# Storing the attention's numerators and sums undivided, features on partitions, and dividing in the output stage

## The chip, the cores and the metric

One core of one Trainium2 chip. The metric is the device time of one execution in microseconds: the median of three runs, and beside it one profiled execution from which all rows below come. Five engines matter: TensorE (matmuls and transposes, PE in the profile, PEld its weight loads), VectorE (DVE), ScalarE (ACT), GpSimd (POOL), and SyncE (SP), which issues all DMAs of this kernel.

## The reference

A transformer block on x of 16 batches, 512 rows, 128 features: 16 heads of 8 features, relative positions clipped at 20, then a gated feed-forward part.

```python
# q, k, v: layernorm(x) @ W.T + b, per head; rk2, rv2: rel_k, rel_v by clipped distance
attn1 = jnp.einsum('bhqd,bhkd->bhqk', q, k)
attn2 = jnp.einsum('bhqd,qkd->bhqk', q, rk2)
attn = jax.nn.softmax((attn1 + attn2) / scale, axis=-1)
w1 = jnp.einsum('bhqk,bhkd->bhqd', attn, v)
w2 = jnp.einsum('bhqk,qkd->bhqd', attn, rv2)
out = (w1 + w2).transpose(0, 2, 1, 3).reshape(B, S, E) @ Wo.T + bo
x = x + out
h = jax.nn.silu(gate) * up          # of layernorm(x)
x = x + h @ wd.T
```

## The kernel before

Three stages run one after the other, each a block that all engines leave together: projections (to about 200 us), attention (to about 1216 us) and output (to the end). Between them, queries, keys, values and the attention's result go through memory.

The attention stage (`stage_attend`) works in 64 units: 16 batches of 4 blocks of 128 query rows; i = 0 to 3 is the block within the batch. A unit has 8 score chunks c, two for each of the 4 key blocks t = c // 2, each chunk of two banks of 512 columns. TensorE writes scores to three banks `b_s` in turn, ScalarE takes the exponential of each bank (L1004, `b_p<-b_s`). Before each bank TensorE waits for `p_ready` of the exponential that frees it, three banks back; in `scores`, where t == i (the diagonal block), it waits for each of the two banks by itself and issues the first bank's work and the row-maximum scores before the second wait, otherwise it waits once for both. Beside each chunk stand the row-maximum scores of two heads of the unit after next (L810, `b_a<-k,q`), whose maxima VectorE takes (L1043).

The unit before is finished during the chunks of the present one. c = 0: the last value products (L901, `b_pv`). c = 1: relative values into the bank `b_mi` (L916), masked by VectorE (L1050, `b_wm`). c = 2: their sums into `b_pv` (L927); ScalarE copies `b_pv` to `b_xt` (L1016), and behind it the transposed guard rows to `b_mt` (L1010). After chunk 3: `output_transposes`, four transposes of `b_xt` back into `b_mi` (L937); VectorE divides: reciprocal of the 16 sums (L1057) and a product (L1062) into `b_xn`; SyncE stores `b_xn` (L721) at the end of its unit, two units behind. In SyncE's queue, per unit: with i = 0 and 1 operand loads of the next batch (L231), each held until a chunk of scores is done; the guard rows of the next unit (L683, two DMAs); more operand loads; with i = 2 the values; then the store.

The output stage (`stage_output`) takes one batch per step, with projection of the batch after. TensorE per step: output projection of the next batch (L1164, `c_py`), three pairs of gate and up products (L1181, L1182), the attention's transposes of the batch after next (L1156, `c_pa`), 12 down products (L1189), transposes of the next batch's normalised rows (L1172). ScalarE copies the transposed attention to `c_aT` (L1220), which the projection reads, and takes the Silu (L1235). VectorE: residual sum (L1251), statistics, hidden products 0 and 1 (L1271), normalisation (L217), hidden product 2, final sum (L1288). GpSimd: the deviation's inverse and the bias addition of the batch after next (L1132). Loads for the batch after next are issued by SyncE once the residual sum has been made.

Of the kernel before, what the change touches and what calls it, by code (L numbers as in the profile page):

```python
# [16 lines left out]
P = 128  # L17
# [38 lines left out]
NQ4 = 4  # L56
# [539 lines left out]
def stage_attend(nc, m, k, d):  # L596
# [18 lines left out]
    names = ("init", "a_ready", "a_used", "half", "s_ready", "p_ready", "w_ready", "w_masked", "pv_ready", "xt_ready", "rd",  # L615
             "mp_ready", "mt_ready", "mt_copied", "xtt_ready", "norm", "m_in",
# [6 lines left out]
    NSR = 2 * SUB  # L623
    NQD = HP * QB
# [50 lines left out]
    with nc.Block() as block:  # L675
        @block.sync
        def _(sp):
# [18 lines left out]

            def unit(at):
# [10 lines left out]
                if at.plus(1).exists():  # L708
                    guard_rows(at.plus(1))
                if ahead:  # L710
                    for c in range(3, (SUB, NLOAD - SUB)[i]):
                        chunk(c)
                        operands(first, range(c + SUB * i, c + SUB * i + 1))
                if i == 2 and at.since(T) and at.plus(T).exists():
                    load_values(sp, k, d, at.it * 2 + at.c // T + 1, (at.c // T + 1) % 2)
                if at.count() == 4 * T:
                    for p in range(2):
                        sp.wait_ge(xo_out[p], 16 * T)
# [8 lines left out]
            for u in (U - 2, U - 1):  # L727
                sp.wait_ge(s["norm"], u + 1)
                sp.dma_start(d["xo"][u], XN[u % 2][:, :]).then_inc(xo_out[u % 2], 16)
# [70 lines left out]
        def _(pe):  # L800
# [133 lines left out]
            def output_transposes(at):  # L934
                pe.wait_ge(s["xt_ready"], at.count(1, 1))
                for g in range(NQ4):
                    ins = nc.tensor.transpose(MI[:, g * P:(g + 1) * P], XT[:, g * P:(g + 1) * P], k["ident"][:, :])  # L937
                ins.then_inc(s["xtt_ready"], 1)

# [40 lines left out]
            pe.wait_ge(s["norm"], U - 1)  # L980
            relative_values(end)
            relative_value_sums(end)
            output_transposes(end)

        @block.scalar
        def _(act):
# [45 lines left out]
        def _(dve):  # L1032
# [21 lines left out]
            def normalise(at):  # L1054
                dve.wait_ge(s["xtt_ready"], at.count(1, 1))
                v = MI[:, :].rearrange("p (n c) -> p n c", c=32)
                nc.vector.reciprocal(RD[:, :], v[:, :, HD]).then_inc(s["rd"], 1)  # L1057
                dve.wait_ge(s["rd"], at.count(1, 1))
                if at.since(2):
                    dve.wait_ge(xo_out[at.c % 2], at.even(1) * 16)  # L1060
                xn = XN[at.c % 2][:, :].rearrange("p (a g d) -> p g a d", a=NQ4, d=HD)
                nc.vector.tensor_tensor(xn, MI[:, :].rearrange("p (g a c) -> p g a c", g=NQ4, a=NQ4)[:, :, :, 0:HD],  # L1062
                                        bc(RD[:, :].rearrange("p (g a) -> p g a", g=NQ4), 3, HD), ALU.mult).then_inc(s["norm"], 1)

# [17 lines left out]
            normalise(end)  # L1082
# [8 lines left out]
def stage_output(nc, m, k, d):  # L1091
# [3 lines left out]
    XA, X, x_in = k["xa"], k["x"], k["rows_in"]  # L1095
    X1 = [m.sb(f"c_x1{p}", [P, T, E]) for p in range(2)]
    XNT = [m.sb(f"c_xnT{p}", [P, S]) for p in range(2)]
    xn, fin, aT = m.sb("c_xn", [P, T, E]), m.sb("c_fin", [P, T, E]), m.sb("c_aT", [P, S])
# [3 lines left out]
    pA, pT, py, po = (m.ps(f"c_p{n}", [P, S]) for n in ("a", "t", "y", "o"))  # L1102
    PG, PU = ([m.ps(f"c_p{n}{p}", [P, S]) for p in range(2)] for n in "gu")
    names = ("xb", "aT", "aTs", "y", "x1", "var", "eps", "rstd", "xn", "xT", "xTs", "gate", "up", "silu", "hid",
# [6 lines left out]
    with nc.Block() as block:  # L1111
        @block.sync
        def _(sp):
            def step(at):
                if at.plus(2).exists():
                    sp.wait_ge(s["x1"], at.count(1, 1))
                    if at.count() == 0:
                        for p in range(2):
                            sp.wait_ge(k["xo_out"][p], 16 * U // 2)
# [8 lines left out]
        def _(pool):  # L1128
            def biased(at):
                x = X[at.c % 2]  # L1130
                pool.wait_ge(x_in[at.c % 2], at.even(1) * 32 + 32)
# [4 lines left out]

            biased(at0(0))
# [12 lines left out]
        def _(pe):  # L1150
            def attention_transposes(at):
                pe.wait_ge(x_in[at.c % 2], at.even(1) * 32 + 32)
                if at.since(1):
                    pe.wait_ge(s["aTs"], at.count())
                for t in range(T):
                    ins = nc.tensor.transpose(pA[:, t * P:(t + 1) * P], XA[at.c % 2][:, t, :], k["ident"][:, :])  # L1156
                ins.then_inc(s["aT"], 1)

            def output_projection(at):
                pe.wait_ge(s["aTs"], at.count(1, 1))  # L1160
                if at.since(1):
                    pe.wait_ge(s["x1"], at.count())
                for t in range(T):
                    ins = nc.tensor.matmul(py[:, t * P:(t + 1) * P], aT[:, t * P:(t + 1) * P], k["wo"][:, :], start=True, stop=True)  # L1164
# [29 lines left out]
            attention_transposes(at0(0))  # L1194
            output_projection(at0(0))
            attention_transposes(at0(1))
            row_transposes(at0(0))

            def step(at):
# [5 lines left out]
                if at.plus(2).exists():  # L1205
                    attention_transposes(at.plus(2))
# [8 lines left out]
        def _(act):  # L1215
            def transposed_attention(at):
                act.wait_ge(s["aT"], at.count(1, 1))
                if at.since(1):
                    act.wait_ge(s["y"], at.count())
                nc.scalar.copy(aT[:, :], pA[:, :]).then_inc(s["aTs"], 1)  # L1220

# [4 lines left out]
            transposed_attention(at0(0))  # L1226
            transposed_attention(at0(1))
            transposed_rows(at0(0))

            def step(at):  # L1230
# [5 lines left out]
                if at.plus(2).exists():  # L1236
                    transposed_attention(at.plus(2))
# [6 lines left out]
        def _(dve):  # L1244
# [27 lines left out]

            residual(at0(0))
            normalise(at0(0))

            def step(at):
# [7 lines left out]
                hidden(at, 2)  # L1284
                dve.wait_ge(s["down"], at.count(1, 1))
# [8 lines left out]
def program(nc, d):  # L1294
    for name, shape, dt in (("qop", (B, PARTS, P, S), BF16), ("kop", (B, PARTS, P, S), BF16),
                            ("v", (B, P, S), F32), ("guard", (B, P, VGW - VW), F32), ("xo", (U, P, E), F32)):
# [57 lines left out]
```

## Time and profile before

| | |
|---|---|
| median of 3 runs | 1385.82 us (1384.87 to 1387.82) |
| the profiled execution | 1384.85 us, span 1383.1 us |
| TensorE busy | 1264.9 us, 91% |
| VectorE busy | 955.0 us, 69% |
| ScalarE busy | 757.8 us, 55% |
| GpSimd busy | 551.3 us, 40% |
| DMA | 79.08 MB, mean 57 GB/s |

A busy share is a mean over three stages of different kind. The page cuts the span in 40 slices of 34.6 us and gives the busy tenths of each; slices 1 to 5 are the projections, 7 to 35 attention, the last five the output stage. A row of the timeline is an instruction or a run of equal ones, with its start and length and, in brackets, how long its engine had been idle and what it waited for. A row of the groups has count, busy time, and the mean length in nanoseconds.

### The profile page before, as it was taken

Reading aid. Unit: us, or ns where it says so; the run is one execution under the profiler, and the core shown is the slowest. Engines: PE = TensorE matmul, PEld = TensorE weight load, DVE = VectorE, ACT = ScalarE, POOL = GpSimd, SP = SyncE. Lnnn points to the kernel's source line nnn. Section 1 sums busy time; section 2 is a strip of 40 time slices with the busy share of each in tenths; the row PEclk is TensorE's granted clock in tenths of the full one; section 3 lists DMA queues with packets and bytes.
Section 4 is the critical chain, followed back from the end, with each engine's and each line's share of the span. In section 5 each row is a group of like instructions: output and inputs, shape, how many; then the busy total and the mean of one; then the engine's idle time right before and its main releaser. Section 6 shows DMA issues by size and latency. Waiting matters only on the chain. (4 is left out here: it accounts for less than half of the span.)

```text
span 1383.1 us, 67607 instructions
## 1 busy us (share of the span) xinstructions
PE 1264.9 (91%) x30680; PEld 937.8 (68%) x30688; DVE 955.0 (69%) x1844; ACT 757.8 (55%) x1413; POOL 551.3 (40%) x983
## 2 busy tenths in 40 slices
PE   4387669999999999999999999999999999979998
PEld 3254437777777777777777777777777777756766
DVE  6499876776766767677767676676777776146664
ACT  4367525565655656555656566565666565623332
POOL 4376623443435343434344343534344443122221
PEclk9789959999999999999999999999999999989999
DMA  4544520111020112011111101111211110113231
GB/s 126 141 168 167 179 60 7 42 33 55 23 55 23 52 32 57 21 54 42 33 49 29 55 20 54 30 47 32 56 35 41 45 32 9 41 41 92 69 92 46
DMA packets 101541, 79.08 MB, mean 57 GB/s; under 512 B 13256, under 2 KB 97032, under 8 KB 101256
## 3 DMA queue, kind: packets, MB, share of 16 engines
q1 hardware_dynamic: 101256, 74.77, 18.3%
q8 instruction: 242, 3.96, 1.3%
q14 instruction: 43, 0.35, 0.1%
HBM read 45.90 MB, written 27.26 MB: 53 GB/s over the span
## 5 line engine op out<-in xcount | busy, mean ns | idle before, releaser
L1043 DVE TENSOR_REDUCE b_mx<-b_a 128x1 f32<-128x512 f32 x1024 | 658.7, 685 | 234.0 <-PE b_a L810 228.7
L1004 ACT ACTIVATE b_p<-b_s 128x512 f32<-128x512 f32 x1024 | 569.8, 595 | 399.3 <-PE b_s L851 313.6
L901 PE MATMUL b_pv<-b_p,vg 128*16 128x128 f32 x8192 | 286.7, 275 | 0.1
L774 POOL TENSOR_TENSOR qd<-q,one 48x512 bf16<-48x512 bf16 x256 | 266.2, 1040 | 28.7 <-POOLq L286 3.8
L751 POOL TENSOR_TENSOR b_np<-vg,one 128x16 bf16<-128x16 f32 x192 | 39.1, 264 | 560.7 <-DVE b_mx L1043 550.4
L851 PE MATMUL b_s<-qd,z 112*128 112x32 bf16 (+1 forms) x6016 | 248.8, 189 | 0.7 <-issue 0.6
L810 PE MATMUL b_a<-k,q 48*128 48x512 bf16 x1024 | 202.8, 393 | 26.8 <-DVE b_mx L1043 11.3
L851 PEld LDWEIGHTS b_s<-qd,z 112*128 112x128 bf16 x6016 | 205.8, 99 | 11.0 <-issue 1.0
L901 PEld LDWEIGHTS b_pv<-b_p,vg 128*16 128x16 f32 x8192 | 196.2, 96 | 21.4 <-issue 0.6
L836 PE MATMUL b_s<-q,k 54*128 54x64 bf16 (+3 forms) x4608 | 188.2, 201 | 6.4 <-issue 2.5
L836 PEld LDWEIGHTS b_s<-q,k 54*128 54x128 bf16 (+1 forms) x4608 | 126.4, 95 | 92.4 <-PE b_s L836 29.2
L810 PEld LDWEIGHTS b_a<-k,q 48*128 48x128 bf16 x1024 | 49.7, 94 | 95.9 <-ACT b_p L1004 39.8
L861 PE MATMUL b_s<-q,k 118*128 118x64 bf16 x2048 | 104.4, 194 | 0.7 <-issue 0.7
L861 PEld LDWEIGHTS b_s<-q,k 118*128 118x128 bf16 x2048 | 76.8, 98 | 30.0 <-issue 30.0
L1050 DVE TENSOR_TENSOR b_wm<-b_mi,wmask 128x512 f32<-128x512 f32 x64 | 44.3, 692 | 65.8 <-PE b_mi L916 65.8
L927 PE MATMUL b_pv<-b_wm,red 128*16 128x128 f32 x2048 | 70.3, 274 | 5.4 <-DVE b_wm L1050 4.9
L916 PE MATMUL b_mi<-b_p,tvd 128*32 128x64 f32 x4096 | 70.6, 221 | 0.0
L362 PE MATMUL a_pr<-relbd,a_parts 128*128 128x320 bf16 x128 | 29.7, 316 | 37.2 <-DVE a_gr L572 37.2
L916 PEld LDWEIGHTS b_mi<-b_p,tvd 128*32 128x32 f32 x4096 | 60.3, 110 | 4.6
L1235 ACT ACTIVATE c_sg<-c_pg 128x512 f32<-128x512 f32 x48 | 28.7, 597 | 54.8 <-PE c_pg L1181 54.8
L927 PEld LDWEIGHTS b_pv<-b_wm,red 128*16 128x16 f32 x2048 | 50.7, 96 | 11.6 <-DVE b_wm L1050 7.7
L362 PEld LDWEIGHTS a_pr<-relbd,a_parts 128*128 128x128 bf16 x128 | 11.8, 111 | 62.7 <-DVE a_gr L572 53.1
(125 smaller groups left out, 1321.8 us busy)
## 6 DMA issues: line engine op xcount, KB each, us to landing
x<-in_x SPq DMA_DIRECT2D x32, 256.0 KB, 3.2
scratch_qop<-a_parts SPq DMA_DIRECT2D x16, 384.0 KB, 2.5
scratch_kop<-a_parts SPq DMA_DIRECT2D x16, 384.0 KB, 3.2
k<-scratch_kop SPq DMA_DIRECT2D x32, 192.0 KB
q<-scratch_qop SPq DMA_DIRECT2D x32, 192.0 KB
scratch_v<-a_vr SPq DMA_DIRECT2D x16, 256.0 KB, 3.2
k<-scratch_kop SPq DMA_DIRECT2D x32, 128.0 KB
q<-scratch_qop SPq DMA_DIRECT2D x32, 128.0 KB
```

Of the source, the lines that this page charges most:

```text
L362: ins = nc.tensor.matmul(PR[t % 2][:, i, 0:H * REL], PB[at.c % 2][:, 0, 0, t * P:(t + 1) * P], k["relbd"][:, i, :], start=True, stop=True)
L774: nc.gpsimd.tensor_tensor(dst, src, one, ALU.mult).then_inc(s["qd_ready"], 1)
L810: nc.tensor.matmul(PA[(n + hp) % NBANK][:, :], Q[p][r, hh, hp, i * P:(i + 1) * P], K[p][r, hh, :], start=True, stop=True).then_inc(s["a_re ...
L836: ins = nc.tensor.matmul(o, lhs, rhs, start=first, stop=True, skip_group_check=True)
L851: ins = nc.tensor.matmul(o, k["z"][0:QROWS, x0:x0 + P], QD[at.c % 2][0:QROWS, heads[0]:heads[-1] + 1, b * QB:(b + 1) * QB], start=False, s ...
L861: nc.tensor.matmul(SC[bank_of(at, 2 * c + n)][:, hh * 64:(hh + 1) * 64], K[p][r, hh, i * P:(i + 1) * P], Q[p][r, hh, :, q0:q0 + 32], start ...
L901: nc.tensor.matmul(PV[32 * a:32 * a + V16, g * P:(g + 1) * P], v[:, 0 if t <= i else 1, t, h, :], PR[at.c % 2][:, t, h, :], start=(t == 0 ...
L916: ins = nc.tensor.matmul(MI[r0:r0 + WB * HD, grp * H * WB:(grp + 1) * H * WB], tab[:, q0 * HD:(q0 + WB) * HD], PR[at.c % 2][:, t, :, qb * ...
L927: ins = nc.tensor.matmul(o, k["red"][:, b, :], w, start=False, stop=True, skip_group_check=True)
L1004: nc.scalar.activation(out, src, ACT.Exp, scale=SCALE).then_inc(s["p_ready"], 1)
L1043: nc.vector.tensor_reduce(MX[v.c % 2][:, h:h + 1], PA[(n + hp) % NBANK][:, :], AX_X, ALU.max, negate=True).then_inc(s["a_used"], 1)
L1050: nc.vector.tensor_tensor(WM[:, :, :, :].rearrange("p g h q -> p (g h) q"), MI[:, :].rearrange("p (n q) -> p n q", q=WB), bc(k["wmask"][:, ...
```

## The change

The attention stage doesn't transpose and doesn't divide. ScalarE's copy of `b_pv` (now two buffers `b_xt`) holds, for each group a of four heads, 8 rows of numerators and one row of sums on partitions 32a to 32a + 8; SyncE stores these nine rows with four DMAs, right behind the guard rows of its unit. The scratch tensor has the layout batch, feature or sum, head, row. The output stage loads the numerators as 128 partitions (feature, head) of 512 rows (`xa`), and the sums, repeated eight times over the partitions, as `xd`. VectorE takes the reciprocal of `xd` (128x512), GpSimd multiplies `xa` by it, and the projection reads `xa` directly; `wo` has its rows reordered on the host to fit. The reciprocal of the batch after next stands behind hidden product 2 in VectorE's order, and GpSimd's product stands ahead of the bias addition.

```diff
@@ stage_attend @@
-    XT = m.sb("b_xt", [P, NQ4 * P])
-    XN = [m.sb(f"b_xn{p}", [P, E]) for p in range(2)]
-    RD = m.sb("b_rd", [P, H])
+    XT = [m.sb(f"b_xt{p}", [P, NQ4 * P]) for p in range(2)]
...
+            def rows_out(at):
+
+                sp.wait_ge(s["xt_ready"], at.count(1, 1))
+                rows = d["xo"][at.it * 2 + at.c // T][:, :, at.c % T * P:(at.c % T + 1) * P]
+                for a in range(NQ4):
+                    sp.dma_start(rows[:, NQ4 * a:NQ4 * (a + 1), :],
+                                 XT[at.c % 2][32 * a:32 * a + HD + 1, :].rearrange("p (g q) -> p g q", g=NQ4)).then_inc(xo_out[at.c % 2], 16)
+
...
                 if at.plus(1).exists():
                     guard_rows(at.plus(1))
+                if at.since(1):
+                    rows_out(at.plus(-1))
...
-                if at.since(2):
-                    sp.wait_ge(s["norm"], at.count(1, -1))
-                    sp.dma_start(d["xo"][bass.ds(at.count(1, -2), 1)].rearrange("o p c -> (o p) c"), XN[at.c % 2][:, :])\
-                        .then_inc(xo_out[at.c % 2], 16)
...
                             if at.since(2):
-                                pe.wait_ge(s["norm"], at.count(1, -1))
-                            else:
-                                pe.wait_ge(s["mt_copied"], 2)
+                                pe.wait_ge(s["w_masked"], at.count(1, -1))
+                            pe.wait_ge(s["mt_copied"], at.count(1, 1))
                             relative_values(before)
...
-                    if c == 3 and before.exists():
-                        if at.plus(1).exists():
-                            pe.wait_ge(s["mt_copied"], at.count(1, 2))
-                        output_transposes(before)
...
             def output_copy(at):
                 act.wait_ge(s["pv_ready"], at.count(1, 1))
-                if at.since(1):
-                    act.wait_ge(s["xtt_ready"], at.count(1))
-                nc.scalar.copy(XT[:, :], PV[:, :]).then_inc(s["xt_ready"], 1)
+                if at.since(2):
+                    act.wait_ge(xo_out[at.c % 2], at.even(1) * NXO)
+                nc.scalar.copy(XT[at.c % 2][:, :], PV[:, :]).then_inc(s["xt_ready"], 1)
...
-                        if c == 3:
-                            normalise(before)
@@ load_rows @@
-    sp.dma_start(k["xa"][p][:, :, :], d["xo"][bass.ds(batch * T, T)].rearrange("t p e -> p t e")).then_inc(k["rows_in"][p], 16)
+    sp.dma_start(k["xd"][p][:, :], bc(d["xo"][batch][HD], 0, HD)).then_inc(k["rows_in"][p], 16)
+    sp.dma_start(k["xa"][p][:, :], d["xo"][batch][0:HD].rearrange("d h s -> (d h) s")).then_inc(k["rows_in"][p], 16)
@@ stage_output @@
+            def divided(at):
+                x = XA[at.c % 2]
+                pool.wait_ge(x_in[at.c % 2], at.even(1) * NIN + NIN)
+                pool.wait_ge(s["inv"], at.count(1, 1))
+                nc.gpsimd.tensor_tensor(x[:, :], x[:, :], XD[at.c % 2][:, :], ALU.mult).then_inc(s["divided"], 1)
+
+            divided(at0(0))
             biased(at0(0))
+            divided(at0(1))
             deviation(at0(0))
             biased(at0(1))
...
                 if at.plus(2).exists():
+                    divided(at.plus(2))
                     biased(at.plus(2))
...
             def output_projection(at):
-                pe.wait_ge(s["aTs"], at.count(1, 1))
+                pe.wait_ge(s["divided"], at.count(1, 1))
...
-                if at.plus(2).exists():
-                    attention_transposes(at.plus(2))
...
-                if at.plus(2).exists():
-                    transposed_attention(at.plus(2))
...
+            def inverse(at):
+                x = XD[at.c % 2]
+                dve.wait_ge(x_in[at.c % 2], at.even(1) * NIN + NIN)
+                nc.vector.reciprocal(x[:, :], x[:, :]).then_inc(s["inv"], 1)
+
+            inverse(at0(0))
+            inverse(at0(1))
             residual(at0(0))
             normalise(at0(0))
...
                 hidden(at, 2)
+                if at.plus(2).exists():
+                    inverse(at.plus(2))
                 dve.wait_ge(s["down"], at.count(1, 1))
```

## Rows read from the trace of the kernel before

**Rows 1.** The page, busy tenths in 40 slices of the span, TensorE.
```profile
PE   4387669999999999999999999999999999979998
```
**Rows 2.** Windows: stretch, length, busy us (instructions) by engine, TensorE clock, DMA share, GB/s.
```profile
1236.26:1245.90 9.64, 9.64 (x54) 6.72 (x53) 6.25 (x19) 2.97 (x5) 2.49 (x3) 1.00 0.29 82
```
**Rows 3.** Waits of TensorE, 260 to 1150 us: total us, times, longest.
```profile
PE b_a L810 <- ACT b_p L1004: 2.9, 14, 0.2
```
**Rows 4.** Groups by form: output, input, count, busy us, mean ns, idle before.
```profile
L937 PE MATMUL b_mi<-ident,b_xt 128*128 128x128 f32 x256 | 41.0, 283 | 3.1 <-ACT b_xt L1016 1.1
...
L1062 DVE TENSOR_TENSOR b_xn<-b_mi,b_rd 128x128 f32<-128x128 f32 x64 | 18.7, 292 | 2.2
...
L1057 DVE RECIPROCAL b_rd<-b_mi 128x16 f32<-128x16 f32 x64 | 16.1, 252 | 20.6 <-PE b_mi L937 20.6
```
**Rows 5.** Timeline (start us, length us), attention, a unit with i = 0.
```profile
711.16 0.64 PE L937 MATMUL b_mi<-ident,b_xt 128*128 128x128 f32 x4
711.35 1.08 ACT L1004 ACTIVATE b_p<-b_s 128x512 f32<-128x512 f32 x2 [0.34 <-PE b_s L851]
712.00 0.39 PE L810 MATMUL b_a<-k,q 48*128 48x512 bf16 x2 [0.20 <-ACT b_p L1004]
```
**Rows 6.** Timeline, the next unit, i = 1.
```profile
726.37 1.33 ACT L1004 ACTIVATE b_p<-b_s 128x512 f32<-128x512 f32 x2 [0.57 <-PE b_s L851]
...
726.90 0.64 PE L937 MATMUL b_mi<-ident,b_xt 128*128 128x128 f32 x4
727.47 0.29 PE L836 MATMUL b_s<-q,k 54*128 54x64 bf16 x8
```
**Rows 7.** Timeline, the unit with i = 2.
```profile
740.33 0.64 PE L937 MATMUL b_mi<-ident,b_xt 128*128 128x128 f32 x4
...
740.90 0.39 PE L810 MATMUL b_a<-k,q 48*128 48x512 bf16 x2
```
**Rows 8.** Timeline, the unit with i = 3.
```profile
756.02 1.09 ACT L1004 ACTIVATE b_p<-b_s 128x512 f32<-128x512 f32 x2
...
756.11 0.66 PE L937 MATMUL b_mi<-ident,b_xt 128*128 128x128 f32 x4
...
756.70 0.29 PE L836 MATMUL b_s<-q,k 51*128 51x64 bf16 x8
```
**Rows 9.** Timeline of SyncE's queue, a unit with i = 1: issue times.
```profile
725.83 1.63 SPq L683 DMA_DIRECT2D q<-b_mt  x2
...
728.24 0.44 SPq L721 DMA_DIRECT2D scratch_xo<-b_xn  x1
```
**Rows 10.** Groups by form, for prices of the output stage.
```profile
L1050 DVE TENSOR_TENSOR b_wm<-b_mi,wmask 128x512 f32<-128x512 f32 x64 | 44.3, 692 | 65.8 <-PE b_mi L916 65.8
...
L478 POOL TENSOR_TENSOR a_qr<-a_qf,a_parts 128x512 f32<-128x512 f32 x16 | 18.5, 1155 | 3.6 <-ACT a_qf L416 3.6
...
L1156 PE MATMUL c_pa<-ident,xa 128*128 128x128 f32 x64 | 10.1, 282 | 1.4 <-PEq L675 1.4
```
**Rows 11.** Timeline of the output stage, two batches.
```profile
1231.86 1.29 DVE L217 TENSOR_SCALAR c_xn<-c_x,c_mv,c_rstd 128x128 f32<-128x128 f32 x4
...
1236.26 1.06 PE L1164 MATMUL c_py<-wo,c_aT 128*128 128x128 f32 x8
...
1241.49 1.02 PE L1182 MATMUL c_pu<-c_xnT,wu 128*128 128x512 f32 x2
...
1241.50 1.85 DVE L217 TENSOR_SCALAR c_xn<-c_x,c_mv,c_rstd 128x128 f32<-128x128 f32 x4
...
1243.27 0.68 DVE L1271 TENSOR_TENSOR c_hh<-c_sg,c_pu 128x512 f32<-128x512 f32 x1
...
1245.90 1.06 PE L1164 MATMUL c_py<-wo,c_aT 128*128 128x128 f32 x8
```
**Rows 12.** Timeline, the beginning of the output stage.
```profile
1215.98 0.63 PE L1156 MATMUL c_pa<-ident,xa 128*128 128x128 f32 x4 [1.43 <-PEq L675]
...
1219.27 0.69 DVE L1251 TENSOR_TENSOR c_x<-c_py,x 128x512 f32<-128x512 f32 x1 [4.09 <-PE c_py L1164]
```

More of the change, by code:

```diff
@@ L614, in stage_attend @@
     MI = m.ps("b_mi", [P, S])
-    names = ("init", "a_ready", "a_used", "half", "s_ready", "p_ready", "w_ready", "w_masked", "pv_ready", "xt_ready", "rd",
-             "mp_ready", "mt_ready", "mt_copied", "xtt_ready", "norm", "m_in",
+    names = ("init", "a_ready", "a_used", "half", "s_ready", "p_ready", "w_ready", "w_masked", "pv_ready", "xt_ready",
+             "mp_ready", "mt_ready", "mt_copied", "m_in",
              "qd_ready", "v_ready", "guard")
@@ L623, in stage_attend @@
     NSR = 2 * SUB
+    NXO = 16 * NQ4
     NQD = HP * QB
@@ L717, in unit @@
                     for p in range(2):
[L718 to L722 removed]
+                        sp.wait_ge(xo_out[p], NXO * T)
             run_all(unit, PER, U)
@@ L726, in _ @@
                 load_rows(sp, k, d, p, p)
-            for u in (U - 2, U - 1):
-                sp.wait_ge(s["norm"], u + 1)
-                sp.dma_start(d["xo"][u], XN[u % 2][:, :]).then_inc(xo_out[u % 2], 16)
+            rows_out(at0(U - 1))
         @block.gpsimd
@@ L932, in guard_transpose @@
                 nc.tensor.transpose(MIB, NP[:, :, :, :].rearrange("p hp c hh -> p (hp c hh)"), idb[:, :]).then_inc(s["mt_ready"], 1)
[L934 to L938, printed above, removed]
             MIB = MI[0:6 * H, 0:P // 2].bitcast(BF16)
@@ L979, in _ @@
             value_products(end, T - 1)
-            pe.wait_ge(s["norm"], U - 1)
+            pe.wait_ge(s["w_masked"], U - 1)
             relative_values(end)
             relative_value_sums(end)
-            output_transposes(end)
         @block.scalar
@@ L1052, in keep_values @@
                                         bc(k["wmask"][:, :], 1, S // WB), ALU.mult).then_inc(s["w_masked"], 1)
[L1054 to L1063, printed above, removed]
             for u, hh in order[:HH + EARLY]:
@@ L1101, in stage_output @@
            "rstd": m.sb("c_rstd", [P, T]), "gap": m.sb("c_gap", [P, 1])}
-    pA, pT, py, po = (m.ps(f"c_p{n}", [P, S]) for n in ("a", "t", "y", "o"))
+    pT, py, po = (m.ps(f"c_p{n}", [P, S]) for n in ("t", "y", "o"))
     PG, PU = ([m.ps(f"c_p{n}{p}", [P, S]) for p in range(2)] for n in "gu")
-    names = ("xb", "aT", "aTs", "y", "x1", "var", "eps", "rstd", "xn", "xT", "xTs", "gate", "up", "silu", "hid",
+    names = ("xb", "inv", "divided", "y", "x1", "var", "eps", "rstd", "xn", "xT", "xTs", "gate", "up", "silu", "hid",
              "down", "fin", "out", "dv")
@@ L1118, in step @@
                         for p in range(2):
-                            sp.wait_ge(k["xo_out"][p], 16 * U // 2)
+                            sp.wait_ge(k["xo_out"][p], 16 * NQ4 * U // 2)
                     load_rows(sp, k, d, at.count() + 2, at.c % 2)
@@ L1150, in _ @@
         def _(pe):
[L1151 to L1157, printed above, removed]
             def output_projection(at):
-                pe.wait_ge(s["aTs"], at.count(1, 1))
+                pe.wait_ge(s["divided"], at.count(1, 1))
                 if at.since(1):
@@ L1163, in output_projection @@
                 for t in range(T):
-                    ins = nc.tensor.matmul(py[:, t * P:(t + 1) * P], aT[:, t * P:(t + 1) * P], k["wo"][:, :], start=True, stop=True)
+                    ins = nc.tensor.matmul(py[:, t * P:(t + 1) * P], XA[at.c % 2][:, t * P:(t + 1) * P], k["wo"][:, :], start=True, stop=True)
                 ins.then_inc(s["y"], 1)
@@ L1215, in _ @@
         def _(act):
[L1216 to L1220, printed above, removed]
             def transposed_rows(at):
@@ L1295, in program @@
     for name, shape, dt in (("qop", (B, PARTS, P, S), BF16), ("kop", (B, PARTS, P, S), BF16),
-                            ("v", (B, P, S), F32), ("guard", (B, P, VGW - VW), F32), ("xo", (U, P, E), F32)):
+                            ("v", (B, P, S), F32), ("guard", (B, P, VGW - VW), F32), ("xo", (B, HD + 1, H, S), F32)):
         d[name] = nc.dram_tensor("scratch_" + name, shape, dt, kind="Internal").ap()
@@ L1307, in program @@
              "x": [m.sb(f"x{p}", [P, T, E]) for p in range(2)], "x_in": [m.sem(f"x_in{p}") for p in range(2)],
-             "xa": [m.sb(f"xa{p}", [P, T, E]) for p in range(2)], "rows_in": [m.sem(f"rows_in{p}") for p in range(2)],
+             "xa": [m.sb(f"xa{p}", [P, S]) for p in range(2)], "xd": [m.sb(f"xd{p}", [P, S]) for p in range(2)],
+             "rows_in": [m.sem(f"rows_in{p}") for p in range(2)],
              "eps": m.sb("eps", [P, 1]), "root": m.sb("root", [P, 1]), "neg": m.sb("neg", [P, 1]), "one": m.sb("one", [P, 1]),
@@ L1337 @@
         "x": a["attn_hidden_states"],
-        "wq": by_d(a["attn_Wq"]).T, "wk": by_d(a["attn_Wk"]).T, "wv": a["attn_Wv"].T, "wo": a["attn_Wo"].T,
+        "wq": by_d(a["attn_Wq"]).T, "wk": by_d(a["attn_Wk"]).T, "wv": a["attn_Wv"].T, "wo": by_d(a["attn_Wo"].T),
         "bq": by_d(a["attn_bq"])[:, None], "bk": by_d(a["attn_bk"])[:, None],
```

12 lines of the change are left out of this document (4 added, 8 removed).

## The prediction

> **What bounds the kernel now.** I read the page first: the busy tenths in 40 slices. TensorE stands at 9 through the attention stage and almost to the end [rows 1]. So I then ask of each stage what ends TensorE's waits. One batch of the output stage, from one output projection to the next, takes 9.64 us: TensorE is busy all of it, VectorE 6.25 us, GpSimd 2.49 us [rows 2]. There TensorE sets the pace and VectorE has 3.4 us to spare. In the attention stage the waits view shows very few waits of TensorE's matmuls, but one regular one: 14 times 0.2 us, before the row-maximum scores, for an exponential of ScalarE [rows 3]. 14 times in 890 us is once in 64 us, that is, once in each batch of four units of about 16 us, so it is a pattern, and the reader should keep it in mind: TensorE and ScalarE hand three score banks back and forth.
>
> **Attention: the transposes that go.** In each of 63 units the change takes away four transposes of 128 columns after the fourth score chunk, and on VectorE a reciprocal and a product (252 and 292 ns) [rows 4]. VectorE's part is worth nothing by itself: in this stretch the waits view names no matmul that waits for a row maximum. TensorE's part lies on the path, but its price is what starts earlier behind it. The next instruction of TensorE is chunk 4, and the code holds it until the bank three back is free, that is, until the first exponential of chunk 3 is done; for the unit whose diagonal block comes in chunk 4 it is the exponential before that. So I took the four kinds of unit (i = 0 to 3) from the timeline.
> - i = 0: the exponentials begin at 711.35 (at once when the scores are ready) and TensorE goes on at 712.00, having waited 0.20 for them [rows 5]. The transposes from 711.16 lie wholly inside this loop. Without them TensorE waits until 712.00 all the same: gain 0. From here I also read the loop's length: 0.65 us from an exponential's start to TensorE's restart.
> - i = 1: exponential at 726.37, so restart possible at 726.37 + 0.65 = 727.02 instead of 727.47: gain 0.45 [rows 6].
> - i = 2: the diagonal one, nothing holds it: 740.33 to 740.90, gain 0.57 [rows 7].
> - i = 3: exponential at 756.02 (ScalarE has copied until then), restart at 756.67 instead of 756.70: gain 0.03 [rows 8].
>
> That is 1.05 us in a batch, times 16: 16.8 us. Nothing is gained or lost by the shift later in a unit, since exponentials and scores move together. The transposes' whole slots would be 0.84 + 0.57 + 0.57 + 0.59 = 2.57 us a batch, 41.1 in all; that is the other end.
>
> **Attention: what is added.** ScalarE's copy now waits for a store of two units earlier, 29 us back (740.33 less 711.16 is two units): nothing. The new wait of the relative values is for a mask product one unit old: nothing. On SyncE one store becomes four, and they move from the unit's end to right behind the guard rows. Behind them is queued, in units with i = 1, the last operand load of the next batch, which the queue takes up when the guard rows are issued, at 725.83 + 1.63 = 727.46. A store like the one before costs the queue 0.44, a guard-row DMA with its more broken pattern 1.63 / 2 = 0.8 [rows 9]; four cost 1.8 to 3.3 us with gaps. I take 2.1, since the new ones are of 9 partitions with rows of four pieces, between the two. TensorE asks for that load at the beginning of the next unit, four chunks before that unit's transposes at 740.33 [rows 7], by my estimate near 734, over 6 us after its issue, and the trace shows no wait for it. 2.1 us of those 6 leave 4 for its flight. So 0; the upper end is the rival at the end. At the stage's end, where the last copy, transposes and product go, the queue has its four stores to issue instead (2.1 us) before the stage can close: I put down +0.4.
>
> **Output stage: the step that decides.** The change removes the four transposes of a batch, 10.1 / 16 = 0.63 us of TensorE [rows 10], and a ScalarE copy, and adds a chain: reciprocal of 128x512 on VectorE, queued behind the third hidden product, then a product of 128x512 on GpSimd, then the projection. GpSimd's product is 1.16 us by the nearest row [rows 10]. The reciprocal of this size isn't in the trace. Its only row is 128x16: 252 ns [rows 4]. Two products that read PSUM take 292 ns for 128 elements [rows 4] and 692 ns for 512 [rows 10]: 400 / 384 = 1.04 ns an element and 159 fixed. If the reciprocal has the same fixed 159, its 16 elements take 93 ns, 5.8 ns each, and 512 take 2.98 + 0.16 = 3.13 us. The lower bound is that the 252 is mostly fixed: 252 + 496 x 1.04 = 0.77 us. The upper one is a fixed part 40 ns smaller, 8.3 ns each: 4.4 us. I take 3.13, since the fixed part of an instruction that reads PSUM, as both do, is then the same.
>
> Now the loop, from the timeline of one batch [rows 11], counted from the projection at 1236.26. The third hidden product ends at 1243.95, 7.69 us later, while the next projection starts at 1245.90. In the changed kernel GpSimd's bias addition runs much earlier in the batch, so the normalisation beside it takes 1.29 again instead of 1.85 us; it ends at 5.24 + 1.29 = 6.53, the third up product is there at 6.25, and the hidden product ends at 7.25. Then: reciprocal r, GpSimd 1.16, two handovers of 0.1 each (the 0.65 less half of 1.08, the length of two exponentials [rows 5]), projection. Period = 7.25 + r + 1.36 = 8.6 + r. The projection stands ahead of the next gate and up matmuls in TensorE's queue, so everything waits for it; what TensorE can do meanwhile, the last third of the down products and the next batch's transposes, ends within 2 us of the hidden product (1245.90 less 1243.95) and covers no more than that. The reciprocal's own load is no limit: the bias addition needed the same batch's loads earlier in the step than the reciprocal will. With r = 3.13 the period is 11.74 instead of 9.64: +2.10, in the 14 batches whose step has an inverse: +29.4 us.
>
> The prologue: the first residual sum begins at 1219.27, 3.29 after the stage's start at 1215.98 [rows 12]. Now two reciprocals stand ahead of it on VectorE, 6.3 us, and the chain through GpSimd takes as long: 3.13 + 1.36, and about 2.0 for the projections (3.29 less 1.3 for transposes and copy): 6.5 in all, +3.2.
>
> **Sum.** -16.8 + 0.4 + 29.4 + 3.2 = +16.2 us. The profiled execution took 1384.85 us (span 1383.1 and 1.75 around it), 1 us under the median of the runs, 1385.82. 1384.85 + 16.2 = 1401.0.
>
> **The rivals.**
> - A cheap reciprocal (the other side, faster). The mechanism is one row: if the 252 ns are fixed cost, r = 0.77, the period 9.4 and no wait takes the place of the transposes: -3.8 in 14 batches, prologue +0.8, attention -16.8, end +0.4: -19.4, 1365.5. Below r = 1.04, where 8.6 + r passes 9.64, the chain adds no wait; the whole change turns from faster to slower at r = 2.1 (14 x 1.06 and 2.1 in the prologue against 16.4). For it: a 16-element instruction is mostly fixed cost everywhere. Against: 252 is above what 16 elements at 1.04 ns and 159 fixed would take, 176, by 76 ns. Chance 0.13. The Trainium skill has a rule that gives this result: Vector Engine (DVE) Microarchitecture Reference, 5.2 Measured stream behaviour on trn2, puts built-in one-source operations at 1.04 ns a column.
> - A half-price reciprocal: the measured one reads PSUM, the new one SBUF, and no row shows whether that changes its rate. At two elements for the time of one, r is near 1.65: period 10.25, +8.6, prologue +1.7: -6.1, 1378.8. A 5% chance.
> - A dear reciprocal, 8.3 ns an element: period 13.0, +47, prologue +5.7: +36, 1421. Chance 0.13.
> - The whole slots of the transposes are saved in attention, 41.1 instead of 16.8, because ScalarE starts its exponentials sooner too: 1376.7. Against it: in i = 0 they start as soon as the scores are there. Chance 0.06.
> - The operand load comes late behind the four stores: TensorE waits up to 1.3 us in 14 batches, 18 us more: 1419. Chance 0.03.
>
> **How the numbers follow.** The forecast's case has 0.60. The predicted time is its 1401.0. Its own range is 1392 to 1410 (r from 2.9 to 3.5: 14 x 0.3 = 4; the attention term by 5). With the dear reciprocal on one side and the full slots and the half-price one on the other, 1376 to 1422 leaves out the cheap reciprocal and little else. A measurement of this kernel can tell 0.2%, 2.8 us, from no change. Faster by more than that: 0.13 + 0.05 + 0.06 less a little, 0.23. Within it: 0.04. Slower: 0.73.
>
> **What would show it.** Right: RECIPROCAL 128x512 near 3.1 us, x16; in the output stage TensorE's projection waiting 2 to 3 us per batch for GpSimd's product, and that for the reciprocal; a period of 11.7 us; in the attention stage no transposes, the wait before the row-maximum scores in i = 0 grown from 0.20 to about 0.7 us, units with i = 2 shorter by 0.57, about 1 us saved per four units. Wrong: a reciprocal under 1.1 us, or attention shorter by over 30 us. I have no term for TensorE's granted clock, 1.00 in that batch [rows 2]; should it fall in the new waits, the output stage is longer still.

## The result and the profile after

The changed kernel takes 1439.3 us (median; 1437.58 to 1441.28), the kernel before 1386.3 beside it: ratio 1.0383, 95% interval 1.0365 to 1.0401. The forecast was slower, 1401, with a range of 1392 to 1410; the time lies above it, and above the wider 1376 to 1422 too. Timed again beside the last experiment, the ratio was 1.0401 (1.0377 to 1.0424). The profiled execution took 1437.58 us, span 1435.9, 52.8 us more than the span before.

The page after has TensorE's busy tenths and its granted clock in 40 slices. It stands against [rows 1]:

```profile
PE   4477579999999999999999999999999995788888
...
PEclk9699769999999999999999999999999998789899
```

Up to the 33rd slice almost nothing has changed for the eye; the 34th and 35th hold the passage to the output stage, and from the 36th on TensorE stands at 8, where the stage had been at 9, with a clock of 8 in two of these five slices. The windows view (stretch, length, busy us by engine with counts, granted clock, DMA share, GB/s) shows it in two stretches of one batch of the output stage, from a projection to the next; it stands against [rows 2]:

```profile
1238.81:1243.21 4.40, 4.40 (x12) 2.44 (x13) 1.94 (x10) 0.60 (x1) 2.01 (x3) 0.61 0.91 209
1243.21:1252.32 9.11, 6.72 (x38) 4.56 (x36) 6.90 (x9) 1.78 (x3) 1.70 (x3) 1.00 0.05 16
```

The period, from one projection to the next, is 13.51 us in place of 9.64. The timeline (start, length) of that batch, against [rows 11]:

```profile
1238.81 1.29 PE L1144 MATMUL c_py<-wo,xa 128*128 128x128 f32 x8 [2.41 <-POOL xa L1120]
...
1239.89 1.92 PE L1161 MATMUL c_pg<-c_xnT,wg 128*128 128x512 f32 x2
...
1243.21 1.02 PE L1161 MATMUL c_pg<-c_xnT,wg 128*128 128x512 f32 x2
...
1245.79 1.11 DVE L217 TENSOR_SCALAR c_xn<-c_x,c_mv,c_rstd 128x128 f32<-128x128 f32 x4
...
1246.90 0.69 DVE L1237 TENSOR_TENSOR c_hh<-c_sg,c_pu 128x512 f32<-128x512 f32 x1
1247.51 3.35 DVE L1242 RECIPROCAL xd<-xd 128x512 f32<-128x512 f32 x1
...
1251.00 1.27 POOL L1120 TENSOR_TENSOR xa<-xa,xd 128x512 f32<-128x512 f32 x1 [7.41 <-DVE xd L1242]
...
1252.32 1.16 PE L1144 MATMUL c_py<-wo,xa 128*128 128x128 f32 x8 [2.39 <-POOL xa L1120]
```

The reader is to see a chain: hidden product, reciprocal, GpSimd's product, projection, and TensorE idle for 2.4 us before the projection. Then a second thing: the first gate product after the wait takes 1.92 us, the later one shown 1.02. The 0.61 in the windows is a mean of both of TensorE's levels, 1.2 and 2.4 GHz; later in the batch it is 1.00.

One of the 14 rounds with such a wait is different, and it is a test of its own. The same 2.39 us of idle time stand before its projection, the DMA share behind it is as high, but the clock stays at 1.00, and the gate product takes 1.02 us:

```profile
1306.37:1310.77 4.40, 4.40 (x16) 2.52 (x17) 2.51 (x11) 1.19 (x2) 2.09 (x3) 1.00 0.91 226
...
1306.37 1.16 PE L1144 MATMUL c_py<-wo,xa 128*128 128x128 f32 x8 [2.39 <-POOL xa L1120]
1307.36 1.02 PE L1161 MATMUL c_pg<-c_xnT,wg 128*128 128x512 f32 x2
```

The next projection begins at 1318.19, so this round takes 11.82 us. Thus the lower clock costs 13.51 - 11.82 = 1.69 us a round, and it is paid behind 13 of the 14 waits. The other four profiles with this wait (the changed kernel again, and three of the experiments below) have one such round each too.

In the attention stage, the waits of TensorE between 260 and 1150 us answer [rows 3] (total us, times, longest):

```profile
PE b_a L813 <- ACT b_p L995: 9.9, 15, 0.7
PE b_s L839 <- ACT b_p L995: 9.7, 14, 0.7
PE b_a L813 <- DVE b_mx L1034: 5.4, 14, 0.4
PE b_pv L930 <- DVE b_wm L1041: 3.7, 14, 0.3
```

14 or 15 times each is once a batch. The last row isn't new: in the kernel before, the same wait (L927 for L1050) came 13 times with 3.4 us, a second regular one that the prediction passes over when it speaks of one. The other three stand where the transposes stood: for an exponential with i = 0 and i = 3, and with i = 2 for a row maximum. The places themselves, i = 0, 1, 2 and 3 in this order, against [rows 5 to 8]:

```profile
708.08 1.09 ACT L995 ACTIVATE b_p<-b_s 128x512 f32<-128x512 f32 x2 [0.34 <-PE b_s L854]
708.73 0.39 PE L813 MATMUL b_a<-k,q 48*128 48x512 bf16 x2 [0.69 <-ACT b_p L995]
...
723.14 1.33 ACT L995 ACTIVATE b_p<-b_s 128x512 f32<-128x512 f32 x2 [0.57 <-PE b_s L854]
723.79 0.29 PE L839 MATMUL b_s<-q,k 54*128 54x64 bf16 x8
...
736.36 2.54 DVE L1034 TENSOR_REDUCE b_mx<-b_a 128x1 f32<-128x512 f32 x4 [0.63 <-PE b_a L813]
...
737.20 0.39 PE L813 MATMUL b_a<-k,q 48*128 48x512 bf16 x2 [0.39 <-DVE b_mx L1034]
...
752.54 1.09 ACT L995 ACTIVATE b_p<-b_s 128x512 f32<-128x512 f32 x2
753.19 0.29 PE L839 MATMUL b_s<-q,k 51*128 51x64 bf16 x8 [0.69 <-ACT b_p L995]
```

From an exponential's start to TensorE's restart it is 0.65 us each time (708.08 to 708.73, 723.14 to 723.79, 752.54 to 753.19), as read before. To compare whole units I use the start of the guard rows' transpose, one in each unit. The least distance from one to the next, 14 or 15 values for each kind (without the first and the last batch where these differ):

| from the unit with i = | before | after | gain |
|---|---|---|---|
| 0 | 14.57 | 14.56 | 0.01 |
| 1 | 14.38 | 13.93 | 0.45 |
| 2 | 15.87 | 15.84 | 0.03 |
| 3 | 18.19 | 18.16 | 0.03 |

So 0.52 us a batch, 8 us in 16. Units with i = 0 are uneven in both kernels, mean 15.08 before and 15.18 after. From the first of these transposes to the last it is 1002.4 us before and 997.5 after. This total is the less certain figure: the changed kernel's second profile has 1000.5, and the profiles of three experiments that leave the attention stage as it is have 998.3, 1001.9 and 1002.3, against a single profile of the kernel before. The span's 52.8 us are then: -1.1 up to the first of them, -4.9 in the units, +1.4 from the last to the beginning of the output stage, and 224.5 less 167.1 = +57.4 in the output stage.

### The profile page after: what moved, and what is told of

It reads as the page before. It is cut to its first block and busy times, and to the rows that moved or that the text cites. A ratio compares the mean times of both kernels' runs of the same rounds, so it can differ in the third digit from the quotient of the medians.

```text
span 1435.9 us, 66986 instructions
## 1 busy us (share of the span) xinstructions
PE 1253.9 (87%) x30360; PEld 917.7 (64%) x30368; DVE 971.6 (68%) x1732; ACT 748.7 (52%) x1397; POOL 572.2 (40%) x999
## 5 line engine op out<-in xcount | busy, mean ns | idle before, releaser
L1120 POOL TENSOR_TENSOR xa<-xa,xd 128x512 f32<-128x512 f32 x16 | 20.2, 1264 | 135.6 <-DVE xd L1242 135.6
L1161 PE MATMUL c_pg<-c_xnT,wg 128*128 128x512 f32 x96 | 61.5, 729 | 0.7 <-ACT c_xnT L1194 0.7
```

What stands on the lines that cost most here:

```text
L1161: nc.tensor.matmul(PG[n][:, :], k["wg"][:, c * P:(c + 1) * P], XNT[at.c % 2][:, :], start=True, stop=True).then_inc(s["gate"], 1)
```

## The experiments

All ran beside the kernel before; an edit is shown against the changed kernel where nothing else is said.

**Half the reciprocal.**

```diff
-                nc.vector.reciprocal(x[:, :], x[:, :]).then_inc(s["inv"], 1)
+                nc.vector.reciprocal(x[:, 0:S // 2], x[:, 0:S // 2]).then_inc(s["inv"], 1)
```

> The changed kernel with each reciprocal of the output stage over half of its columns, 256 of 512 (the other half is multiplied by the undivided sum: half of the division is left out). Theory: the loss is the reciprocal's length on the path from the third hidden product to the projection, paid twice, once as it is and once by TensorE's clock, which goes down to its lower level in the 2.4 us wait. The two measured lengths, 252 ns for 16 elements and 3342 for 512, give 6.2 ns an element, so 1.75 us here. TensorE's wait falls from 2.4 to 0.8 us; if the clock then stays up, the period falls from 13.5 to 10.4 us and the time from 1439 to about 1393; if it still falls, to about 1414. Rival: the projection waits for the loads (the sums repeated over the partitions) or for the handovers, not for the reciprocal: above 1430.

Measured: 1394.3 us, ratio 1.0068 (1.0040 to 1.0096). A later batch in the timeline:

```profile
1283.71 1.75 DVE L1242 RECIPROCAL xd<-xd 128x256 f32<-128x256 f32 x1
...
1286.92 1.16 PE L1144 MATMUL c_py<-wo,xa 128*128 128x128 f32 x8 [0.79 <-POOL xa L1120]
```

The projection before this one began at 1276.70, so the period is 10.22 us. Halving an instruction of 3.35 us takes 3.3 us from the period, twice what it is shorter by: the other half is the clock, which in these rounds stays at 1.00 (even the gate product right after the one wait of 1.22 us took 1.02 us). The projection waits for the reciprocal, not for the loads.

**No division.** `inverse`, `divided` and their waits go; the projection waits for the loads.

```diff
             def output_projection(at):
-                pe.wait_ge(s["divided"], at.count(1, 1))
+                pe.wait_ge(x_in[at.c % 2], at.even(1) * NIN + NIN)
...
-                if at.plus(2).exists():
-                    inverse(at.plus(2))
```

> The changed kernel without reciprocal and product in the output stage (the division is left out; all loads and stores stay). Theory: the output stage then runs at TensorE's pace without the four transposes, a period of 9.2 us, its clock at the upper level: about 1374, which also shows what the attention part is worth alone. Rival that the three loads of a batch or the stores hold the stage: over 1400.

Measured: 1380.7, ratio 0.9961 (0.9937 to 0.9984). The period is 9.21 us as expected, so the three loads of a batch don't hold the stage. The total is 7 above the 1374. Most of it lies ahead of the output stage, where the code is the changed kernel's: the stage begins at 1216.9 us here and at 1211.4 there, and from first to last guard transpose it is 1001.9 us here and 997.5 there. The changed kernel alone moves by 3.0 us between its two profiles.

**TensorE kept busy while it waits.**

```diff
                 if after.exists():
                     row_transposes(after)
+                if at.plus(2).exists():
+                    for n in range(20):
+                        nc.tensor.transpose(pF[:, n % T * P:(n % T + 1) * P], k["ident"][:, :], k["ident"][:, :])
```

> The changed kernel with 20 transposes of a constant into a free bank, 2.2 us by the 0.11 us of one, put behind the row transposes of each output-stage step that has a reciprocal, so that TensorE is busy while it would wait for GpSimd's product. Theory: TensorE's clock stays at its upper level, projection and first gate and up products take 1.0 instead of 1.9 us, the period falls from 13.5 to about 11.9: 1417. Rival: the slow matmuls behind the wait have another cause than the wait (a port shared with VectorE's reciprocal or GpSimd's product): no change or slower, 1439 or more.

Measured: 1421.7, ratio 1.0270 (1.0240 to 1.0300). One batch, windows view and timeline:

```profile
1255.65:1267.47 11.82, 11.61 (x68) 8.50 (x68) 8.72 (x19) 2.38 (x4) 3.72 (x5) 1.00 0.36 90
...
1255.65 1.16 PE L1145 MATMUL c_py<-wo,xa 128*128 128x128 f32 x8 [0.21 <-POOL xa L1121]
...
1256.65 1.02 PE L1162 MATMUL c_pg<-c_xnT,wg 128*128 128x512 f32 x2
...
1264.91 2.35 PE L1190 MATMUL c_pf<-ident 128*128 128x128 f32 x20
```

Reciprocal, product and loads are as in the changed kernel; only TensorE isn't idle. The gate product is back at 1.02 us, the clock at 1.00, the period 13.51 less 1.69, in every round. So 13 x 1.69 = 22 us of the loss are the clock's. In these rounds it falls only behind idle time of TensorE, and a shared port or the loads aren't the cause: the DMA share over the 4.4 us behind the projection is 0.84 here, and it was 0.91 both behind the slow matmuls of the changed kernel and behind the fast ones of its one different round. The whole kernel gained less than that, 16 us by the ratios, and missed the 1417 that was expected: the output stage is 22.9 us shorter (201.6 for 224.5), but it begins 6.1 us later in this profile, behind stages of the same code.

**The transposes put back**, after chunk 3, their result unused, VectorE's part left out.

```diff
+                    if c == 3 and before.exists():
+                        if at.plus(1).exists():
+                            pe.wait_ge(s["mt_copied"], at.count(1, 2))
+                        output_transposes(before)
```

> The changed kernel with the four transposes of a unit put back into TensorE's queue behind chunk 3, their result unused, VectorE's division still gone. Theory: in three of the four units of a batch TensorE waits where the transposes stood, for an exponential (i = 0, 3) or for a row maximum (i = 2), so they cost 0.5 us a batch: 8 us more, 1447. Rival, the price of the slots: 2.57 us a batch, 41 us, 1480.

Measured: 1448.6, ratio 1.0454 (1.0422 to 1.0486), 9 us above the changed kernel. The guard transposes' least distances are again those of the kernel before, 14.57, 14.39, 15.87 and 18.19 (the second without the last batch). Of the three kinds of wait only the old one is left:

```profile
PE b_a L813 <- ACT b_p L1005: 2.9, 14, 0.2
```

The 41 us that the slots would be worth are refuted; VectorE's reciprocal and product have no part in the attention stage's pace.

**Shorter row maxima, in both kernels.**

```diff
-PA[(n + hp) % NBANK][:, :], AX_X, ALU.max
+PA[(n + hp) % NBANK][:, 0:S // 2], AX_X, ALU.max
```

> The changed kernel with VectorE's row maxima taken over 256 of the 512 scores (half of the maximum is left out), 0.42 instead of 0.69 us each. Theory: in units with i = 2 TensorE waits 0.39 us for a maximum where the transposes stood; this goes, 0.4 to 0.5 us a batch, 6 to 8 us, beside 5 to 10 us that shorter maxima bring in the first units of either kernel: 1424 to 1428. Rival: the wait in i = 2 is for the exponentials as in the others: only the 5 to 10 us, and a wait of the same length for ScalarE in its place.

> The kernel before with VectorE's row maxima over 256 of the 512 scores (half of the maximum is left out). It is the counterpart of the same edit in the changed kernel, which shortened the units with i = 2 by 0.27 us. Theory: here the transposes cover the time for which TensorE would wait for a maximum, so i = 2 stays at 15.87 us from guard rows to guard rows, and only the first units gain, up to 4 us: 1382 to 1386. Rival: shorter maxima are good in every unit of either kernel: i = 2 shorter here too.

Measured: 1435.2 (ratio 1.0348, 1.0324 to 1.0373) and 1381.3 (0.9952, 0.9936 to 0.9967). The least distance for i = 2 goes from 15.84 to 15.57 in the changed kernel and stays at 15.87 in the kernel before. The waits for `b_mx` leave the table between 260 and 1150 us and no other takes their place. So the maxima hold i = 2 only where the transposes don't cover them. The gain, 0.27, is less than the wait of 0.39, because a maximum still holds the place; what is left of the wait is 0.12 us, too short for the table. The timeline of the changed kernel with shorter maxima shows it:

```profile
607.30 0.76 DVE L1034 TENSOR_REDUCE b_mx<-b_a 128x1 f32<-128x256 f32 x2 [1.17 <-PE b_a L813]
...
607.87 0.39 PE L813 MATMUL b_a<-k,q 48*128 48x512 bf16 x2
```

The first of the two maxima, 0.42 us long, ends at 607.72, and TensorE goes on 0.15 later. In the changed kernel it is 736.36 + 0.69 = 737.05 and again 0.15 to 737.20. The 0.27 are the difference of the two lengths. The totals say little here: both kernels gain some 5 us, in the changed one less than the 11 to 15 expected, since its units with i = 0 came out at a mean of 15.40 in that profile.

**The reciprocal before the repetition.** The sums of a batch are loaded as 128x64, inverted in the attention stage, stored; `xd` is loaded from there.

```diff
+def invert_sums(nc, dve, k, batch):
+
+    dve.wait_ge(k["su_in"], 16 * (batch + 1))
+    nc.vector.reciprocal(k["su"][:, :], k["su"][:, :]).then_inc(k["ri_done"], 1)
...
-    sp.dma_start(k["xd"][p][:, :], bc(d["xo"][batch][HD], 0, HD)).then_inc(k["rows_in"][p], 16)
+    sp.dma_start(k["xd"][p][:, :], bc(d["ri"][batch], 0, HD)).then_inc(k["rows_in"][p], 16)
```

> The changed kernel with the reciprocal taken before the sums are repeated: for each batch the 8192 sums are loaded as 128x64, inverted by VectorE during the attention stage (for the last batch in the output stage), stored, and the output stage loads the inverses, repeated over the partitions. Everything is computed. Theory: a reciprocal of 64 columns takes 0.16 + 64 x 6.2 ns = 0.56 us, once a batch and beside TensorE's work; the output stage runs at TensorE's pace, period 9.2 to 9.4 us, with the clock up, at most 0.2 us a batch given back because GpSimd's product stands beside the normalisation: 1381 to 1385. Rival: the extra load, store and VectorE instruction collide with the attention stage or the loads of the output stage: over 1390.

Measured: 1382.3, ratio 0.9975 (0.9959 to 0.9991). The groups by form show the price:

```profile
L1088 DVE RECIPROCAL su<-su 128x64 f32<-128x64 f32 x16 | 8.7, 543 | 0.0
```

The same quotients, 8.7 us of VectorE in place of 53.4. The period of the output stage is 9.21 us, as without any division, so none of it is on the path.

**Value products moved into the wait**, on top of the early reciprocal, and alone in the kernel before; the diff is the same in both.

```diff
-                    if c == 4:
-                        value_products(at, 0)
+                    if c in (3, 4):
+                        value_products(at, 0, range(H // NQ4)[2 * (c - 3):2 * (c - 2)])
```

> The kernel with the compact reciprocal, and half of the value products that stand behind score chunk 4 moved behind chunk 3, where the transposes were. Theory: TensorE's wait there (0.69 us in units with i = 0 and 3, 0.39 with i = 2) is for another engine's finishing time, so 0.5 us of useful work in it costs nothing, and it shortens chunk 4 by as much, except where chunk 4 then has too little cover for its own exponential (some 0.15 us): 0.4 + 0.4 + 0.3 less 0.3 in all, about 0.8 us a batch, 13 us: 1370. Rival: chunk 4 loses what chunk 3 gains: no change.

> The kernel before with the same half of the value products moved behind chunk 3 (and behind the transposes). Theory: there the transposes already cover the wait; only the 0.20 us with i = 0 can go, and chunk 4 may lose 0.15: within 3 us of the kernel before, 1386. Rival: the move is good by itself, whatever stands in the gap: 1375 or less, and then the gain of the moved products in the changed kernel isn't the transposes' wait.

Measured: 1376.8, ratio 0.9927 (0.9906 to 0.9948), and 1401.3, ratio 1.0109 (1.0091 to 1.0127). Both differ from what was expected, and the least distances from guard transpose to guard transpose say where:

| i = | compact reciprocal | and moved products | kernel before | with moved products |
|---|---|---|---|---|
| 0 | 14.72 | 14.65 | 14.57 | 14.62 |
| 1 | 13.93 | 14.23 | 14.38 | 14.71 |
| 2 | 15.84 | 15.51 | 15.87 | 15.99 |
| 3 | 18.17 | 17.93 | 18.19 | 18.49 |

The values for i = 0, whose units are uneven, are the weakest of them. In the first pair the waits behind chunk 3 are gone, but only 5.5 us are gained of 12 to 13 expected; by the table it is 0.34 us a batch, 5.4 in all. With i = 1, where nothing was waiting, chunk 3 grows by the products' 0.53 us and chunk 4 gives back 0.24. Chunk 4, now with half of its products, is itself too short for its exponential: up to the next chunk it takes 1.31 us, a round of the loop with ScalarE, in place of 1.55 (i = 0), and 1.69 in place of 1.93 (i = 1). In the kernel before, chunk 3 grows by 0.56 us with i = 1, 2 and 3, and by 0.29 with i = 0, where the old wait takes the rest. Chunk 4 gives back 0.24, and 0.43 with i = 2. That is 0.80 us a batch, 13 of the 15 us. Neither theory nor rival had foreseen this loss. It shows the same thing as the transposes' case from the other side: what an instruction costs here depends on whether its chunk is shorter or longer than the exponential's round.

**The stores at the unit's end** in SyncE's queue, behind the operand loads; alone, and together with the two edits before.

```diff
-                if at.since(1):
-                    rows_out(at.plus(-1))
                 if ahead:
                     for c in range(3, (SUB, NLOAD - SUB)[i]):
...
                 if at.count() == 4 * T:
                     for p in range(2):
-                        sp.wait_ge(xo_out[p], NXO * T)
+                        sp.wait_ge(xo_out[p], NXO * (T - 1))
+                if at.since(1):
+                    rows_out(at.plus(-1))
```

> The changed kernel with the four stores of a unit at the end of the unit in SyncE's queue, behind the operand loads, where the one store stood before. Nothing is left out. Theory: the stores cost the path nothing where they are, so no change: 1439 plus or minus 3, and units with i = 0 are as uneven as in the changed kernel (mean 15.2 us for a least of 14.56). Rival: the four stores ahead of the operand loads delay loads or instruction fetches, and that is the 3 us by which the attention stage gains less than 0.5 us a batch would give: 1436 or less, i = 0 nearer to 14.6.

> The kernel with the compact reciprocal and the moved products, and the four stores of a unit at the end of the unit in SyncE's queue. Everything is computed. Theory: the three edits touch different places, so their gains add: the 1376.8 of the first two less the 3 to 5 us that the late stores seemed to bring, about 1373. Rival: the late stores' gain was the difference of two sets of runs and not of the kernels: 1377 again.

> The changed kernel as it is, timed beside the other on one chip, to see how far its ratio to the kernel before moves from one set of runs to another. If the late stores' 1.0346 is a gain of the kernel, this one stays at 1.038; if the sets differ by as much, it may come out at 1.035.

Measured: 1434.4, ratio 1.0346 (1.0322 to 1.0370), for the changed kernel with late stores; 1369.6, ratio 0.9868 (0.9852 to 0.9885), for all three edits together; the changed kernel again 1.0401 (1.0377 to 1.0424). The last interval doesn't touch the first; the one from the changed kernel's first timing, 1.0365 to 1.0401, overlaps with it by 0.0005. The interval of all three edits doesn't touch that of the two, 0.9927 (0.9906 to 0.9948). So in two pairs the place of the stores is worth 0.4 to 0.6%, 5 to 8 us, and it adds to the other two edits. I had expected no change, and of the three together 1373. The profiles agree on where it is: from first to last guard transpose 995.1 us with late stores against 997.5 and 1000.5, and 991.5 against 1002.1. The least distances with i = 1, 2 and 3 are the same, so it is the unevenness of the units that shrinks, not a step that all of them share. What in the stores' place does it is open. The time in which TensorE waits for nothing that the trace names was 4.5 us with late stores and 6.2 and 7.9 in the changed kernel's two profiles (sums between 200 and 1170 us), and 7.1 against 13.8 in the other pair. In both that is less than the gain, and whether the four stores delay TensorE's instruction fetches is a guess that wasn't tried.

## Why the prediction was wrong

- The direction and the mechanism in the output stage were right: the reciprocal stands on the path from the third hidden product to the projection, and half a reciprocal or none takes the loss away.
- The reciprocal's price: 3.13 predicted, 3.34 measured (mean 3342 ns). Of the two rules of the Trainium skill, neither gives this price. The four lengths, 252, 543, 1744 and 3342 ns for 16, 64, 256 and 512 elements, lie at 6.2 ns an element and 0.15 us fixed. The Trainium skill, VectorE: DVE Perf Modes, Specifications, gives a clock of 0.96 GHz; by that 6.2 ns are 6 cycles (an estimate), not the 8 that the prediction took from the repeat count, which the page doesn't call a time for an element. The 1.04 ns a column of the Trainium skill, Vector Engine (DVE) Microarchitecture Reference, 5.2, don't hold for this instruction: the measured price is six times that. The reading with the fixed part of the neighbouring rows was the nearest.
- The period: 11.74 predicted, 13.51 measured. From the hidden product's end to the projection 4.73 instead of 4.49 (reciprocal 0.21, GpSimd's product 1.27 instead of 1.16, handovers 0.07 less). From the projection to the hidden product's end 8.78 instead of 7.25: this 1.53 is the step that failed. With the clock up, as in the filler's kernel, the same stretch takes 7.10, so the clock's part is all of it and more: 1.69 us behind 13 of the 14 waits, 22 us. The prediction had no term for the clock, put it at nothing and named it only in its last sentence, though it had put an idle gap of about 2.5 us into every batch. Its own profile has matmuls at the lower level behind gaps: 0.50 granted between 1217.5 and 1227.6 us, after four gaps of 0.7 to 1.4 us, where the projection takes 1.95 us for a later 1.06:

```profile
1217.28 1.95 PE L1164 MATMUL c_py<-wo,c_aT 128*128 128x128 f32 x8 [0.68 <-ACT c_aT L1220]
```

- The prologue: 3.65 instead of 3.2. The attention stage's end: 1.4 instead of 0.4; I can't say why, and in the other profiles with this code it is between 1.0 and 2.6.
- Attention: 16.8 predicted, 8 in the least distances, 4.9 in the units as run. i = 0, 1 and 3 came as predicted, 0, 0.45 and 0.03. The step that failed is "i = 2: nothing holds it". The row-maximum scores have three banks of their own, and `row_pair` waits for `a_used`, the maximum that frees one. The trace of before has the row from which to read it:

```profile
740.03 1.29 DVE L1043 TENSOR_REDUCE b_mx<-b_a 128x1 f32<-128x512 f32 x2 [0.63 <-PE b_a L810]
```

The first of these maxima ends near 740.72, and 0.15 later, at 740.87, TensorE can go on; it did at 740.90, so 0.03 was to be gained, as measured, and not 0.57. I had asked only for the exponentials, because the waits view named no wait for a maximum: a wait that other work covers isn't in that view. The further 3 us are unevenness between units, which moves by as much between profiles of the same code and is greater with the stores where the changed kernel has them.
- The stores were priced at nothing and cost 5 to 8 us. The rival had them delay an operand load, but TensorE waits for none in the waits view; how they cost it stays open.
- Sum of the terms: 16.2 predicted; the output stage 24.8 more (57.4 for 29.4 + 3.2, of which 22 are the clock's), the attention units 11.9 more (-4.9 for -16.8, of which 9 are i = 2), its end 1.0 more, and 1.1 less before the units: 52.8 measured.
- The direction wasn't luck: it rests on the reciprocal's price and place, and both were nearly as predicted. The clock alone doesn't account for the miss: without its 22 us the kernel would have taken some 1416, still above the range, by the gain in attention that didn't come.

## What to carry to other kernels

Work taken out of a busy engine's queue is worth the distance to the next thing that would have stopped it, and there can be a second stop behind the first: go through every wait of the next instruction in the code, those that the trace doesn't show too, because other work covers them. When a change puts an idle gap into TensorE's queue once in each round (here 2.4 us in 13.5), price the matmuls behind the gap at the lower clock as well, not only the gap. And invert sums before they are repeated: the price goes by columns per partition, here 64 instead of 512.

## What the runs showed of the hardware

TensorE's clock: behind idle gaps of 2.4 us, 13 of 14 in each of five profiles, some 3 us of matmuls ran at the lower level (1.92 us for what takes 1.02), and behind the fourteenth none did. In steady rounds with gaps of 0.8 us, and once 1.2, none did, nor behind the 2.4 us when they were filled with 20 transposes. The reciprocal costs 6.2 ns a column, and the 16-element one, which reads the matmul banks, lies on the same line as the three that read the memory on the chip. The normalisation of four times 128 columns, 1.29 to 2.17 us in the rounds before in which GpSimd's bias addition stood beside it, took 1.11 where nothing did.
